# Delta-rule attention: scores taken out of the solve loop, computed in 32x64 array tiles over parity-masked keys, and kept raw in SBUF

## The chip, the cores and the metric

The kernel runs on one core of a Trainium2 chip. The metric is the device time of one execution in microseconds (us), as the median of several runs. TensorE multiplies matrices and writes to PSUM (8 banks of 512 float32 columns in 128 partitions); VectorE and ScalarE read PSUM and SBUF; GpSimd works on SBUF alone; SyncE issues transfers. The engines run side by side and wait for each other through semaphores.

## The reference, cut to what matters

The program is a decoder of two layers over 16 sequences of 64 tokens with 256 features. The change touches only the attention of the second layer, with 16 heads of 16 features, chunks of 16 positions and 64 positions in all:

```python
def step(S, inp):                       # one chunk of CHUNK positions (here all 64 of a sequence)
    K, V, bt = inp
    A = jnp.tril(jnp.einsum('bhik,bhjk->bhij', K, K) * bt[:, :, None, :], -1)
    rhs = V - jnp.einsum('bhck,bhkv->bhcv', K, S)
    Vn = jax.scipy.linalg.solve_triangular(eye + A, rhs, lower=True)
    ...
v, _state = _kernel_regression(k, v, beta)
k = k * beta[..., None]
scores = jnp.einsum('bqhd,bkhd->bhqk', q, k) * scale
scores = jnp.where(mask, scores, -jnp.inf)          # mask: lower triangle
attn = jax.nn.softmax(scores, axis=-1)
out = jnp.einsum('bhqk,bkhd->bqhd', attn, v).reshape(b, n, d)
return out @ Wo
```

So there are two things that meet only at the end: the triangular solve that makes the new values v, and the causal softmax over the scores of q and k, which needs nothing of the solve.

## The kernel before, in words

Everything is written by hand, engine by engine: each engine's code is a list of instructions in program order, with waits on semaphores, and nothing reorders it. Only the part between the turned queries and keys and the values is touched.

*Keys by keys.* TensorE turns queries and keys tile by tile (8 tiles of 128 tokens, two sequences each), ScalarE copies them out as `qt1` (queries) and `kbt1` (keys times beta), and TensorE multiplies keys by keys into the matrix of the solve, `na1`. While this goes on, VectorE scales the keys of the next tile (L2409, L2410), and copies half of the products. GpSimd makes the first three of the "keys by head" `kb1` (L737): a product of the keys with a head mask, eight heads wide, one for each of 16 work items w (w = 2j + k, tile j, feature half k), in three buffers.

*Inverses.* The 16x16 diagonal blocks are turned (L1327), copied out by ScalarE (L1918), and inverted by substitution (`invert1`, L416 and L418), half of them on VectorE, half on GpSimd, which first clears their place `ti1` (L754). Each half goes to memory and comes back in another layout (SyncE, L622 and L626). ScalarE fills two blocks of units into `na1` (L1927), GpSimd a third (L763).

*Solve loop.* 16 solve steps t (four chunks of 16 positions x four groups): `rest_of_chunk` (L1383, what earlier chunks give), `own_heads` on VectorE (a masked product), `solved_chunk` (L1397, times the inverse), then copies of the result back into `xv1`, three by ScalarE (L1945) and one by VectorE (L2446). Into the same loop are woven the 16 items of the softmax: `scores1` (L1350 puts the causal mask into a bank through a bf16 identity, L1353 adds the scores of 64 queries with eight heads wide of masked keys), `softmax1` on VectorE (maximum L2429 and subtraction L2430, both from PSUM), `exp1` on ScalarE (L1932), `turn_probs1` (L1362, four transposes) and `keep_probs` on ScalarE (L1939) into `pt1`. Four items run ahead of the loop, with matmuls that only keep TensorE's clock up (L816); scores use one bank, turned probabilities one.

*After the loop* TensorE puts the values in order (L1429) and multiplies probabilities by values (`values1`, L1444). Later the cross attention uses, for its own scores (`scores5`, L1478), tiles of 32 rows x 64 columns, 32 of them for a tile of tokens.

A float32 matmul stands as two records in the trace, so 16 records of L1383 are eight matmuls.

## Time and profile before

| | us |
|---|---|
| median of 3 runs | 1045.49 |
| lowest and highest of them | 1042.62 and 1056.3 |
| the profiled execution | 1040.52 |
| its span, first to last instruction | 1038.6 |
| TensorE (matmul) busy | 958.0 (92%) |
| VectorE busy | 541.3 (52%) |
| ScalarE busy | 362.9 (35%) |
| GpSimd busy | 213.7 (21%) |

Busy time is summed over stages that have different limits, so a share says little about one of them. A busy TensorE is also one whose matmuls only keep the clock up. The chain that ended last, 68% TensorE and 21% VectorE over the whole program, has to be read stretch by stretch; here the stretch is that from about 530 to 652 us.

### The profile page before, as it was taken

Reading aid. Unit: us, or ns where it says so; the run is one execution under the profiler, and the core shown is the slowest. Engines: PE = TensorE matmul, PEld = TensorE weight load, DVE = VectorE, ACT = ScalarE, POOL = GpSimd, SP = SyncE. Lnnn points to the kernel's source line nnn. Section 1 sums busy time; section 2 is a strip of 40 time slices with the busy share of each in tenths; the row PEclk is TensorE's granted clock in tenths of the full one; section 3 lists DMA queues with packets and bytes.
Section 4 is the critical chain, followed back from the end, with each engine's and each line's share of the span. In section 5 each row is a group of like instructions: output and inputs, shape, how many; then the busy total and the mean of one; then the engine's idle time right before and its main releaser. Section 6 shows DMA issues by size and latency. Waiting matters only on the chain.

```text
span 1038.6 us, 18579 instructions
## 1 busy us (share of the span) xinstructions
PE 958.0 (92%) x7302; PEld 594.0 (57%) x7302; DVE 541.3 (52%) x1083; ACT 362.9 (35%) x729; POOL 213.7 (21%) x259
## 2 busy tenths in 40 slices
PE   7799899999989999999888899878899999999995
PEld 3665543333458899997554467746554444444453
DVE  2589788988441110113788677758663232332325
ACT  2334536666522223333477245245230000000002
POOL 6011100000012222312125842730000111111110
PEclk9999999999989999999999999999799999999998
DMA  5000330000345555645130201230105033332001
GB/s 210 1 3 1 119 136 2 2 2 2 122 149 211 164 185 177 185 148 171 48 42 1 81 2 42 83 145 3 51 13 128 0 93 93 92 93 88 6 0 42
DMA packets 28602, 81.43 MB, mean 78 GB/s; under 512 B 10068, under 2 KB 17372, under 8 KB 22500
## 3 DMA queue, kind: packets, MB, share of 16 engines
q1 hardware_dynamic: 26308, 74.20, 21.9%
q0 software_dynamic: 2208, 6.03, 1.9%
q8 instruction: 60, 0.98, 0.4%
q14 instruction: 26, 0.21, 0.1%
HBM read 70.62 MB, written 8.55 MB: 76 GB/s over the span
## 4 chain that ended last, share of the span: by engine, by line
PE 68%; DVE 21%; ACT 4%; issue 3%; POOL 2%; DMA 1%; DVEq 0%; SPq 0%; ACTq 0%; POOLq 0%
PE psum L1588 9%; PE psum L1164 8%; PE psum L1176 8%; DVE arena L2185 5%; PE psum L1592 3%; PE psum L878 3%; PE psum L1383 3%; PE psum L1618 3%; PE psum L1576 3%; PE psum L1622 3%; PE psum L1554 2%; PE psum L1062 2%; DVE arena L2102 2%; DVE arena L2101 2%; PE psum L1613 2%
## 5 line engine op out<-in xcount | busy, mean ns | idle before, releaser
L2034 ACT ACTIVATE arena<-psum 128x512 f32<-128x512 f32 (+1 forms) x32 | 19.0, 593 | 219.5 <-PE psum L1592 219.5
L1842 ACT ACTIVATE arena<-psum,arena 128x128 f32<-128x128 f32 x184 | 52.4, 368 | 115.4 <-PE psum L1164 78.5
L1588 PE MATMUL psum<-arena 128*128 128x512 f32 (+1 forms) x192 | 90.6, 608 | 0.5 <-DVE arena L2653 0.5
L805 POOL TENSOR_TENSOR arena<-arena 128x512 f32<-128x512 f32 (+1 forms) x32 | 40.4, 1264 | 234.5 <-ACT arena L2034 234.5
L2185 DVE TENSOR_REDUCE arena<-psum 128x2 f32<-128x512 f32 x128 | 82.5, 688 | 11.0 <-PE psum L1008 9.5
L1164 PE MATMUL psum<-arena 128*128 128x128 f32 x736 | 86.8, 276 | 0.5 <-DVE arena L2328 0.5
L1164 PEld LDWEIGHTS psum<-arena 128*128 128x128 f32 x736 | 84.0, 192 | 3.4 <-issue 2.7
L1176 PE MATMUL psum<-arena 128*128 x368 | 83.4, 378 | 0.0
L2328 DVE COPY arena<-psum 128x256 f32<-128x256 f32 x23 | 9.7, 424 | 136.5 <-PE psum L1149 86.0
L1819 ACT ACTIVATE arena<-psum 128x1024 f32<-128x1024 f32 x64 | 65.3, 1024 | 30.4 <-PE psum L1030 27.1
L1176 PEld LDWEIGHTS psum<-arena 128*128 128x128 f32 x368 | 67.9, 189 | 9.0
L2653 DVE TENSOR_TENSOR arena<-arena,psum 128x512 f32<-128x512 f32 (+1 forms) x32 | 22.1, 689 | 86.9 <-POOL arena L805 86.4
L1588 PEld LDWEIGHTS psum<-arena 128*128 128x128 f32 (+1 forms) x192 | 33.1, 185 | 55.2 <-issue 53.5
L816 PE MATMUL psum<-arena 128*128 128x512 f32 (+1 forms) x118 | 50.9, 554 | 0.0
L1008 PE MATMUL psum<-arena 32*128 32x256 f16 x256 | 44.5, 276 | 5.8 <-DVE arena L2185 2.7
L728 POOL DMA_INDIRECT returned<-arena x23 | 22.7, 987 | 123.5 <-DVE arena L2344 123.5
L2636 DVE TENSOR_TENSOR arena<-psum,arena 128x512 f32<-128x512 f32 x32 | 22.1, 692 | 49.7 <-issue 45.8
L737 POOL TENSOR_TENSOR arena<-arena 128x512 f32<-128x512 f32 x32 | 32.9, 1054 | 45.9 <-ACT arena L1900 27.4
L878 PE MATMUL psum<-arena 64*128 64x256 f32 x256 | 33.1, 399 | 6.5 <-DVE arena L2132 5.9
L1062 PE MATMUL psum<-arena 128*32 128x256 f32 x512 | 35.1, 393 | 0.6 <-ACT arena L1819 0.5
L1592 PE MATMUL psum<-arena 64*128 64x512 f32 (+1 forms) x96 | 34.4, 625 | 0.0
L816 PEld LDWEIGHTS psum<-arena 128*128 128x128 f32 (+1 forms) x118 | 19.3, 169 | 26.2 <-issue 25.8
(357 smaller groups left out, 1764.2 us busy)
## 6 DMA issues: line engine op xcount, KB each, us to landing
arena<-in_w SPq DMA_DIRECT2D x31, 1024.0 KB, 9.9
arena<-in_experts SPq DMA_DIRECT2D x8, 1248.0 KB, 6.0
arena<-mixed SPq DMA_DIRECT2D x16, 256.0 KB
arena<-mixed SPq DMA_DIRECT2D x8, 512.0 KB, 9.3
arena<-returned SPq DMA_DIRECT2D x8, 256.0 KB, 4.5
kept<-arena SPq DMA_DIRECT2D x2, 1024.0 KB, 7.8
arena<-kept SPq DMA_DIRECT2D x2, 1024.0 KB, 5.9
arena<-in_w_ffn SPq DMA_DIRECT2D x1, 1152.0 KB, 5.1
```

Source lines behind the costliest of these rows:

```text
L805: do(pool.tensor_tensor(out=g6[rows, 2 * half + i, :], in0=g6[rows, 2 * half + i, :], in1=scale6[rows, f % BUFS, cols], op=ALU.mult), scaled6)
L816: pe.matmul(bank(spare), eye, wide(eye, 1, BANK // P), start=True, stop=True)
L878: last = pe.matmul(replicated(u, p)[:, g * D:(g + 1) * D], w[rows, g, :], qr[rows, u % 2, i, :], start=(i == 0), stop=(i == 1), tile_posit ...
L1008: last = pe.matmul(bank(u % 2)[:, tc * D:(tc + 1) * D], stack["q"][r0:r1, b, g, tc * P:(tc + 1) * P], stack["k"][r0:r1, b, g, :], start=Tr ...
L1062: last = pe.matmul(bank(6)[32 * q:32 * q + 32, 0:D], vx[:, b, sc, q, 32 * g:32 * g + 32], ptx[:, (n + q // 2) % 4, q % 2, sc, :], start=(g ...
L1164: last = pe.matmul(bank(n)[:, i * P:(i + 1) * P], w1_tile[:, r % 2, k, features], xst[:, r % 2, k, :], start=(k == 0), stop=(k == KC - 1))
L1176: last = pe.matmul(bank(4 + r % 2)[:, 0:D], hidt[:, r % 2, ic * P:(ic + 1) * P], w2v[:, bass.ds(e, 1), ic, :], start=(ic == 0), stop=(ic = ...
L1588: pe.matmul(out, e[w][:, k, :], xe6[:, half, k, :], start=(k == 0), stop=False)
L1592: mid_ps.by(pe.matmul(out, qb6[r0:r1, n // 2 % 2, q0:q0 + m], aw6[r0:r1, half, :], start=False, stop=True))
L1819: ptx_ready.by(act.activation(ptx[:, n % 4, :, :, :].rearrange("p a b c -> p (a b c)"), bank(2 + 2 * (n % 2), 2), ACT.Exp, scale=float(DHX ...
L1842: last = act.activation(hidt[:, r % 2, ic * P:(ic + 1) * P], bank(n)[:, i * P:(i + 1) * P], ACT.Gelu, bias=b1_tile[:, r % 4, ic:ic + 1])
L2185: ax_max.by(dve.tensor_reduce(nmx[:, b % 2, :, h], bank(u % 2).rearrange("p (t s) -> p t s", t=2), AX.X, ALU.max, negate=True))
```

## The change

Scores are now made two items at a time (n = 0 to 7, tile j), right after the diagonal blocks are out, in banks 0 to 5 by turns. Instead of keys masked by head and eight heads wide, GpSimd makes two copies of the keys, `kwp1[0]` and `kwp1[1]`, each masked by the parity of the head; an array tile of 32 feature rows holds two heads, and the parity picks one of them. A score is then a matmul of 32 rows, 64 queries and 64 keys, at a tile position of the array. ScalarE copies every bank of raw scores to SBUF (`raw1`): the second eight items into their own places of `pt1`, which are free by then, the first eight into the room beyond the arena and next to `xv1`. In the loop, VectorE takes maximum and subtraction from there, two items ahead; turned probabilities get two banks; the fourth copy of a solved chunk goes from VectorE to ScalarE; and GpSimd instead of ScalarE fills the unit block of chunk 2. The items are taken in the order 8 to 15, 0 to 7. The keep-clock matmuls of this stretch are gone.

```diff
+        kwp1 = [key_half(kw_at), key_half(ARENA + BEYOND - KC * B * S)]
+
+        def raw1(w):
+            if w >= NT:
+                return pt1[:, w, :]
+            at = ARENA + w * BANK if w < NT - 2 else xv1_at - (NT - w) * BANK
+            return arena.t[:, at:at + BANK]
...
-        GROUPS, EARLY_W = 4, 4
+        GROUPS, W_ORDER = 4, [*range(NT, 2 * NT), *range(NT)]
...
-            sp.wait_ge(a1_ps.sem, 2 * NT)
+            sp.wait_ge(a1_ps.sem, NT)
             sp.dma_start(w_x1, a["w_xattn1"]).then_inc(loaded["w_xattn1"].sem, 16)
...
+            def keys_by_parity(j):
                 pool.wait_ge(ft_sb.sem, 2 * j + 1)
...
+                for k in range(KC):
+                    for e in range(2):
+                        last = pool.tensor_scalar(
+                            kwp1[e][:, k, j * P:(j + 1) * P].rearrange("p (a i) -> p a i", i=CH),
+                            kbt1[k][:, 2 * j:2 * j + 2, :, 0:CH].rearrange("p b c i -> p (b c) i"),
+                            c["parity"][:, e:e + 1], None, ALU.mult)
                 kb1_ready.by(last)
...
-            for w in range(3):
-                keys_by_head(w)
+            for j in range(NT - 1):
+                keys_by_parity(j)
...
+            keys_by_parity(NT - 1)
             pool.wait_ge(nd1_sb.sem, nd1_sb.base + 2 * CHUNKS)
             invert1(pool, do, pool_step, 1)
...
-            for w in range(3, 2 * NT):
-                keys_by_head(w)
+            for chunk in (2, 3):
+                rows = slice(32 * chunk, 32 * chunk + 32)
+                do(pool.tensor_copy(na1[rows, chunk, :, :].rearrange("p u (h i) -> p (u h) i", i=CH),
+                                    wide(c["ident"][rows, 32 * chunk:32 * chunk + CH], 1, B * KC * 8)), unit_pool)
...
+                for g in range(2):
+                    pe.matmul(bank(2 * (n % 3) + g), ident1, wide(causal1, 1, 8), start=True, stop=False,
+                              skip_group_check=True)
+                for i in range(2):
+                    at = slice((2 * j + i) * S, (2 * j + i + 1) * S)
+                    for k in range(KC):
+                        for r in range(2):
+                            to = ((i * KC + k) * 2 + r) * S
+                            for quad in range(4):
+                                g, e = divmod(quad, 2)
+                                rows = slice(32 * quad, 32 * quad + 32)
+                                last = pe.matmul(bank(2 * (n % 3) + g)[64 * e:64 * e + 64, to:to + S], qt1[rows, k, at],
+                                                 kwp1[r][rows, k, at], start=False, stop=True,
+                                                 tile_position=(32 * quad, 64 * e), skip_group_check=True)
                 a1_ps.by(last)
...
-            for w in range(EARLY_W):
-                scores1(w)
-                if w == 0:
-                    keep_clock(16, 5)
-                if w >= 1:
-                    keep_clock(2, 5, ident1)
-                    turn_probs1(w - 1)
+            pe.wait_ge(causal_ready.sem, causal_ready.base + 1)
+            pe.wait_ge(nd1_sb.sem, nd1_sb.base + 2 * CHUNKS)
+            for n in range(NT):
+                scores1(n)
             pe.wait_ge(xv1_in.sem, xv1_in.base + 16 * 2 * CHUNKS)
+            pe.wait_ge(raw_sb.sem, raw_sb.base + 2 * NT)
             for t in range(SOLVES + 1):
-                w = EARLY_W + t
                 if t < SOLVES:
                     rest_of_chunk(t)
-                if w < 2 * NT:
-                    scores1(w)
                 if t >= 1:
                     solved_chunk(t - 1)
-                if w <= 2 * NT:
-                    turn_probs1(w - 1)
...
+                if t < SOLVES:
+                    turn_probs1(t)
...
+            act.wait_ge(xv1_in.sem, xv1_in.base + 16 * 2 * CHUNKS)
+            for n in range(2 * NT):
+                act.wait_ge(a1_ps.sem, n // 2 + 1)
+                raw_sb.by(act.activation(raw1(W_ORDER[n]), bank(2 * (n // 2 % 3) + n % 2), ACT.Copy))
+            act.wait_ge(gather_dve.sem, gather_dve.base + 4)
+            unit_act.by(act.activation(na1[32:64, 1, :, :].rearrange("p u (h i) -> p (u h) i", i=CH),
+                                       wide(c["ident"][32:64, 32:32 + CH], 1, B * KC * 8), ACT.Copy))
...
-                for q in range(3):
+                for q in range(4):
                     xv_act.by(act.activation(group_units(t, q)[32 * chunk:32 * chunk + CH],
...
+                if t < SOLVES:
+                    keep_probs(t)
+                if t + 2 < 2 * NT:
+                    exp1(t + 2)
...
+            for n in range(2):
+                softmax1(n)
+            for t in range(SOLVES):
+                own_heads(t)
+                if t + 2 < 2 * NT:
+                    softmax1(t + 2)
```

Where this puts the instructions: TensorE first, at the head of the solve loop. In these rows `wct_sb` is the semaphore of `own_heads`, `kb_ready` that of the copied `xv1`, `ceb_sb` that of the raw scores in SBUF (before: of VectorE's solved copy). Before, an iteration of the loop:

```order
L1383 MATMUL psum<-arena 128x128 [waits wct_sb]
L1383 MATMUL psum<-arena 128x128 x3
L1350 MATMUL psum<-arena 128x512 [waits sm_ready,kb1_ready]
L1353 MATMUL psum<-arena 64x512 x2
L1397 MATMUL psum<-arena 16x128 [waits wct_sb]
L1397 MATMUL psum<-arena 16x128 x3
L1362 MATMUL psum<-arena 128x128 [waits pt_sb,sm_exp]
L1362 MATMUL psum<-arena 128x128 x3
```

Now, from the last pair of scores (L1362 is now the mask, L1372 the tiles) into the loop (L1402 rest, L1382 turned probabilities, L1415 solved):

```order
L1362 MATMUL psum<-arena 128x512 [waits ceb_sb,kb1_ready]
L1362 MATMUL psum<-arena 128x512
L1372 MATMUL psum<-arena 64x64 x32
L1402 MATMUL psum<-arena 128x128 [waits ceb_sb,kb_ready]
L1402 MATMUL psum<-arena 128x128 x7
L1382 MATMUL psum<-arena 128x128 [waits sm_exp]
L1382 MATMUL psum<-arena 128x128 x3
L1402 MATMUL psum<-arena 128x128 x8
L1415 MATMUL psum<-arena 16x128 [waits wct_sb,tst1_in_0]
L1415 MATMUL psum<-arena 16x128 x3
```

The mask and the scores stand ahead of the loop, and an iteration is rest, solved, turned probabilities. Turned probabilities 0 now stand behind rest 0 and ahead of rest 1.

ScalarE from the copied diagonal blocks on. Before (L1918 diagonal blocks, L1927 units, L1932 exponentials, L1939 kept probabilities):

```order
L1918 ACTIVATE arena<-psum 128x4x4x16 [waits r1_ps] x8
L1927 ACTIVATE arena<-arena 32x4096 [waits yx_read]
L1927 ACTIVATE arena<-arena 32x4096 [waits yx_ps]
L1932 ACTIVATE arena<-arena 128x512 [waits sm_ready] x2
L1939 ACTIVATE arena<-psum 128x512 [waits pt_ps]
```

Now (L1930, L1936 raw scores, L1938 units, L1943 exponentials, L1950 kept probabilities, L1956 solved copies):

```order
L1930 ACTIVATE arena<-psum 128x4x4x16 [waits r1_ps] x8
L1936 ACTIVATE arena<-psum 128x512 [waits a1_ps,kb_ready]
L1936 ACTIVATE arena<-psum 128x512 [waits a1_ps] x15
L1938 ACTIVATE arena<-arena 32x4096 [waits yx_read]
L1943 ACTIVATE arena<-arena 128x512 [waits sm_ready] x2
L1950 ACTIVATE arena<-psum 128x512 [waits pt_ps]
L1943 ACTIVATE arena<-arena 128x512 [waits sm_ready]
L1956 ACTIVATE arena<-psum 16x2x128 [waits cnt_ps]
L1956 ACTIVATE arena<-psum 16x2x128 x3
```

Sixteen raw copies stand ahead of the one unit block that is left, and both ahead of the first exponential.

## Rows read from the trace of the kernel before

**Rows 1.** The chain in order of time: start us, us, engine, line, records.
```profile
600.42 1.98 PE psum L1383 x16
602.40 0.32 PE psum L1350
602.72 1.01 PE psum L1353 x4
603.73 0.56 PE psum L1397 x16
604.29 0.59 PE psum L1362 x4
...
631.03 1.79 PE psum L1383 x16
632.81 0.22 PE psum L1350
...
652.19 5.46 PE psum L1429 x64
```

**Rows 2.** Timeline of the inverses' time: start us, us, engine, line, operation, idle before.
```profile
559.90 7.27 ACT L1927 ACTIVATE arena<-arena 32x4096 f32<-32x4096 f32 x2
...
560.02 0.29 POOL L416 TENSOR_TENSOR arena<-arena 128x60 f32<-128x60 f32 x1 [8.03 <-ACT arena L1918]
560.02 0.38 PE L1350 MATMUL psum<-arena 128*128 128x512 bf16 x1 [1.12 <-ACT arena L1918]
...
561.33 14.00 PE L816 MATMUL psum<-arena 128*128 128x512 f32 x32
...
577.17 0.69 DVE L2430 TENSOR_TENSOR arena<-psum,arena 128x512 f32<-128x512 f32 x1
...
578.01 0.58 PE L1350 MATMUL psum<-arena 128*128 128x512 bf16 x1 [2.68 <-DVE arena L2430]
...
578.52 1.98 PE L1353 MATMUL psum<-arena 128*64 128x512 f32 x4
...
579.06 0.38 SPq L626 DMA_DIRECT2D arena<-inverse  x1
```

**Rows 3.** The two transfers of L626, from issue to landing.
```profile
DMA to landing us min/median/max: 4.2/4.3/4.3
```

**Rows 4.** Stretches: length, PE, PEld, DVE, ACT, POOL busy, granted clock, DMA.
```profile
578.00:579.00 1.00, 0.99 (x3) 0.37 (x5) 0.00 (x0) 0.53 (x1) 0.83 (x3) 0.53 0.52 213
582.00:583.00 1.00, 0.82 (x5) 0.29 (x5) 0.03 (x1) 0.94 (x2) 1.00 (x1) 1.00 1.22 327
```

**Rows 5.** ScalarE by shape, 560 to 655: count, busy us, mean ns, idle before.
```profile
L1945 ACT ACTIVATE arena<-psum 16x256 f32<-16x256 f32 x48 | 17.9, 374 | 27.9 <-PE psum L1397 27.1
...
L1932 ACT ACTIVATE arena<-arena 128x512 f32<-128x512 f32 x16 | 10.0, 624 | 18.5 <-DVE arena L2430 18.5
L1939 ACT ACTIVATE arena<-psum 128x512 f32<-128x512 f32 x16 | 9.5, 593 | 2.5 <-PE psum L1362 2.2
```

**Rows 6.** Timeline of the cross attention's scores, TensorE.
```profile
697.81 1.99 PE L1478 MATMUL psum<-arena 32*64 32x64 f32 x64
...
705.92 1.16 PE L1478 MATMUL psum<-arena 32*64 32x64 f32 x64
```

**Rows 7.** Timeline while keys are turned; last row: GpSimd by shape, 500 to 560.
```profile
531.34 6.50 POOL L737 TENSOR_TENSOR arena<-arena 128x512 f32<-128x512 f32 x6 [27.43 <-ACT arena L1900]
...
535.00 0.75 DVE L2409 TENSOR_TENSOR arena<-arena 128x256 f32<-128x256 f32 x1
...
535.78 1.15 DVE L2410 TENSOR_TENSOR arena<-arena 128x256 f32<-128x256 f32 x1
...
538.29 0.42 DVE L2409 TENSOR_TENSOR arena<-arena 128x256 f32<-128x256 f32 x1
...
547.15 1.80 POOL L754 MEMSET arena<- 128x2048 f32 x1 [9.32 <-PE psum L1292]
...
L749 POOL CAST arena<-arena 128x128 bf16<-128x128 f32 x1 | 0.3, 289 | 0.1
```

More of the change, by code:

```diff
@@ L339, in build @@
         kbt1 = [arena.take(B, CHUNKS, 32), ctok.rearrange("p j d -> p (j d)").rearrange("p (b c i) -> p b c i", c=CHUNKS, i=32)]
[L340 removed]
+        kw_at = arena.at
+        arena.take(3, 2, 8, S)
         xv1_at = arena.at
@@ L729, in _ @@
                                             ys[:, q % 2, :], None).then_inc(ys_out[q % 2].sem, 16)
-            def keys_by_head(w):
-                j, k = divmod(w, 2)
+            def keys_by_parity(j):
                 pool.wait_ge(ft_sb.sem, 2 * j + 1)
-                if w >= 3:
-                    pool.wait_ge(a1_ps.sem, w - 2)
-                for i in range(2):
-                    b = 2 * j + i
-                    last = pool.tensor_tensor(out=kb1[:, w % 3, i, :, :].rearrange("p h (c i) -> p h c i", i=CH),
-                                              in0=wide(kbt1[k][:, b, :, 0:CH], 1, 8),
-                                              in1=wide(wide(c["headmask1"], 2, CH), 2, CHUNKS), op=ALU.mult)
+                for k in range(KC):
[4 more added lines that the diff above has]
+                            c["parity"][:, e:e + 1], None, ALU.mult)
                 kb1_ready.by(last)
@@ L1355, in scores1, with turn_probs1 @@
                 a1_ps.by(last)
-            def turn_probs1(w):
-                pe.wait_ge(sm_exp.sem, w + 1)
-                if w >= 1:
-                    pe.wait_ge(pt_sb.sem, w)
+            def turn_probs1(n):
+                pe.wait_ge(sm_exp.sem, n + 1)
+                if n >= 2:
+                    pe.wait_ge(pt_sb.sem, n - 1)
                 for i in range(4):
-                    last = pe.transpose(bank(7)[:, i * P:(i + 1) * P], sm1[:, w % 2, i * P:(i + 1) * P],
+                    last = pe.transpose(bank(6 + n % 2)[:, i * P:(i + 1) * P], sm1[:, n % 2, i * P:(i + 1) * P],
@@ L2421, in _, with softmax1 @@
             invert1(dve, do, dve_step, 0)
-            def softmax1(w):
-                dve.wait_ge(a1_ps.sem, w + 1)
-                if w >= 2:
-                    dve.wait_ge(pt_ps.sem, w - 1)
-                sm = sm1[:, w % 2, :].rearrange("p (h t) -> p h t", t=S)
-                scores = bank(6).rearrange("p (h t) -> p h t", t=S)
-                do(dve.tensor_reduce(mx1[:, w % 2, :], scores, AX.X, ALU.max))
-                do(dve.tensor_tensor(out=sm, in0=scores, in1=wide(mx1[:, w % 2, :], 2, S), op=ALU.subtract),
+            def softmax1(n):
+                dve.wait_ge(raw_sb.sem, raw_sb.base + n + 1)
+                if n >= 2:
+                    dve.wait_ge(pt_ps.sem, n - 1)
+                sm = sm1[:, n % 2, :].rearrange("p (h t) -> p h t", t=S)
+                scores = raw1(W_ORDER[n]).rearrange("p (h t) -> p h t", t=S)
+                do(dve.tensor_reduce(mx1[:, n % 2, :], scores, AX.X, ALU.max))
+                do(dve.tensor_tensor(out=sm, in0=scores, in1=wide(mx1[:, n % 2, :], 2, S), op=ALU.subtract),
                    sm_ready)
```

100 lines of the change are left out of this document (30 added, 70 removed).

## Prediction

> **What bounds the kernel now.** I read the chain that ended last in order of time, then the timeline of the same stretch, then groups by shape. In the solve loop, which ends where L1429 starts at 652.19 us, the chain is TensorE without a gap: every iteration is five pieces that follow each other [rows 1]. An early one is 1.98 (L1383, the rest of a chunk) + 0.32 (L1350, the causal term) + 1.01 (L1353, the scores) + 0.56 (L1397, the solved part) + 0.59 (L1362, the turned probabilities) = 4.46 us. From the chunk with 96 rows on, L1383 is 1.79 and L1350 0.22, so 4.16. ScalarE and VectorE are not the bound there: per iteration they run three L1945 copies, one L1939 and one L1932 (3 x 0.37 + 0.59 + 0.62 = 2.3 us) [rows 5], and four operations of 0.69 such as L2430 [rows 2] with one short copy.
>
> Before the loop TensorE has nothing useful to do: it does scores 0 at 560.02, then 14.00 us of keep-clock matmuls (L816), sits 2.68 us idle, and comes back only when VectorE has finished its inverse and the first softmax [rows 2]. So the place of free TensorE time is 561 to 578, and the place where TensorE is short is the loop. The change moves work from the second to the first.
>
> **The change, part by part.**
>
> *Scores out of the loop.* Twelve iterations lose L1350 + L1353: eight of 1.33 and four of 1.23 us, 15.6 us of pure path. The four scores ahead of the loop, with their turns, also go; what takes their place is worked out below as a timetable.
>
> *Scores in the new form.* A pair of old scores becomes two L1350 and 32 tiles of 32 rows x 64 columns. The trace has this tile form in the cross attention (L1478, 64 records for 32 tiles): 1.16 us at full clock, 1.99 at a low one [rows 6]. A pair is 0.32 + 0.22 + about 1.1 = 1.65 us, against 2 x 1.33 before. Eight pairs from 560.02 (the wait for L1918's last copy is unchanged) end at 573.2. Their three pairs of banks are emptied by ScalarE at 2 x 0.59 = 1.2 us a pair [rows 5], less than 1.65, so it keeps up; the last two copies end at 574.4, and TensorE waits for them.
>
> The Trainium skill, "TensorEngine Tiling (Array Packing)", Restrictions and Gotchas, says that different row tiles cannot access one PSUM bank simultaneously; here two row tiles share each bank, in different partition halves. By the 1.01 us of L1353 for 512 columns a tile of 64 is 0.11 to 0.13; if the two on a bank took turns, I estimate 16 x 0.11 = 1.7 us instead of 1.1 for the tiles of a pair, turn 1 would end 3 us later, and the sum below would give about 19 us instead of 22. L1478 writes its banks in the same way and shows 1.16, so by the row I leave the turn-taking out; what no row shows is the same form accumulating on top of L1350's result.
>
> *Start of the loop.* Rest 0 runs 574.4 to 576.4; it needs neither inverse nor softmax. VectorE's inverse 0 is unchanged, and so its first maximum starts behind it and its first subtraction ends at 577.86 as before [rows 2]. ScalarE does the unit block of chunk 1 first, 3.6 us (half of the 7.27 of two), so it is free at 578.0; exp 0 ends at 578.6. TensorE has then been idle for 2.2 us. Before, after an idle 2.68 us, it came back at 1.2 GHz (granted clock 0.53 at 578 to 579, 1.00 from 582), and L1353 took 1.98 instead of 1.01 [rows 2, 4]. I take the same: turn 0 to 579.8, rest 1 to about 583. Solved 0 needs the first inverse back from memory: its load is issued at 579.06 and lands 4.3 us later, at 583.4 [rows 2, 3]. So the slow clock is covered by that wait, and solved 0 (0.56) and turn 1 (0.59) end at 584.6.
>
> *The loop.* Then rest + solved + turn: 1.98 + 0.56 + 0.59 = 3.13 us for t = 2 to 7 (18.8), and 1.79 + 1.15 = 2.94 for t = 8 to 14 (20.6); rest 15 and solved 14 another 2.35: 626.3. Behind it ScalarE has four copies, one keep of probabilities, four copies: 8 x 0.39 + 0.6 = 3.8 us, so L1429 starts at 630.1. Before it starts at 652.19 [rows 1]. **The sum is 22.1 us.**
>
> *Who else could set the pace.* ScalarE now has 4 x 0.39 + 0.61 + 0.64 = 2.8 us an iteration, since the fourth copy came over from VectorE. VectorE has 4 x 0.72 = 2.9. Both lie just under 2.94. The margin is thin, but what they feed has slack: softmax t+2 and exp t+2 have two iterations, a solved chunk's copy has four. If waits between engines make either 3.2 long, the loop loses about 0.2 x 14 = 3 us.
>
> *Reading raw scores from SBUF.* No row shows a VectorE maximum or subtraction of 128x512 from there; PSUM sources cost 0.69 each. I take 0.69 for both. Above it lies what VectorE showed beside GpSimd, next part; below zero nothing speaks for.
>
> *Keys by parity.* GpSimd makes them in 28 pieces of 128x128 while the queries are turned (531 to 547) and four more at about 552, and does nothing for them in the loop. The six old products took 6.50 us there, 1.08 each for 512 elements of two inputs; a quarter of that is 0.27, and a GpSimd cast of 128x128 took 0.29 [rows 7]. I take 0.3, 28 pieces 8.4 us, and call 0.6 the upper end. The clearing of ti1 (L754) waited 9.32 us and the inverse behind it another 8.03 [rows 2, 7], so up to 0.6 a piece this is covered; above it inverse 0 would be pushed. But VectorE's two scaling products (L2409, L2410), 0.42 each when left alone, took 0.75 and 1.15 at 535, when GpSimd was at its six products [rows 7]. That cost 1.06 us, on the chain. Now GpSimd works through that whole phase in short pieces. If every pair of VectorE's seven later products lost 1.06, that is 7.4 us; if a short piece blocks only briefly, the 1.06 comes back. I take nothing, and both ends go into the range.
>
> The Trainium skill, "SBUF — State Buffer", Who interferes with whom, says that a VectorE operation with two SBUF inputs contends with a GpSimd instruction that reads SBUF, whole instruction by whole instruction, and one with a single SBUF input does not. The rows at 535 agree. By this rule the new subtraction, now with both inputs in SBUF, contends too: softmax 2 and 3 fall on GpSimd's two unit blocks (3.6 us each from 579.5), and I estimate up to 2 us of delay for each, which the wait for the inverse and the slack of two iterations would hide.
>
> *SyncE.* The next stage's weights wait for a1_ps at half the count, so they load before the loop instead of near its end, behind the inverse's loads. Nobody waits for them either way. Nothing downstream of L1429 changes.
>
> **Rivals.**
> - *Slow tiles.* The scores run at the low clock or take turns on the banks. At half clock a pair is 1.99 [rows 6] and about 0.9 for the two L1350, 2.9 us; eight end at 583.2, their copies at 584.4, the unit block at 588.0, turn 0 at 589.3, and the loop's regular part starts 8 us later: 14 us of gain, 1031. Against it: the keep-clock matmuls are replaced by work that is as dense, and L1478 at full clock.
> - *VectorE or ScalarE sets the pace*, by contention with GpSimd in the key phase (up to 7.4) or the thin margin in the loop (3): gain 12 to 19, about 1029. For it: the 0.75 and 1.15, and 2.9 against 2.94.
> - *Slower than before.* TensorE stays at 1.2 GHz after the idle time ahead of turn 0, through the loop. All of the 43 us at half speed cost 43, so the time would be 1045.5 + 21; it decides once more than 44 us of half-speed work, some 22 us lost, come together. Against it: in the trace of before full clock was back by 582 with TensorE far from full.
> - *More than the sum*: the 1.06 comes back and the inverse lands earlier: 25 us or more, below 1020.
>
> **How the numbers follow.** The profiled execution took 1040.5 us (span 1038.6), so the sum gives 1018.4 for it. The median shown is 1045.49, 5 us above; I take the gain off that: 1023. Chances: the forecast (gain 18.5 to 25, 1020 to 1027) 0.65; slow tiles 0.10; another engine sets the pace 0.17; slower 0.03; more than the sum 0.05. Two per cent, about what a measurement of this kernel can tell from no change, are 20.9 us, 1024.6: just beside the forecast. Of the forecast's 0.65 I put 0.45 above it, since the sum is 22.1 with few free terms; with the last case that is 0.50 faster, 0.46 within, 0.04 slower. The range 1017 to 1032 leaves out the slower case, the worst of the contention and noise of the median.
>
> **What would show it.** In the profile after: eight pairs of L1350's successor and 32 tiles at 1.65 us from 560 to 573; an idle TensorE at 576 to 578.6 with a granted clock near 0.5 behind it; solved 0 waiting for the load until 583.4; iterations of 3.13 and 2.94 with no gap; L1429's successor at 630. Wrong would be: tile groups of 1.7 us or more, VectorE's products at 533 to 546 well above 0.42, subtractions above 0.69, or idle TensorE in the loop.

## The result, and the profile after

The changed kernel takes 1043.44 us (median of 18 runs, 1035.80 to 1048.67); the kernel before, run in turn with it, takes 1048.30 (18 runs, 1042.46 to 1056.30). The ratio is 0.9949, with an interval of 0.9924 to 0.9974. So the change gains half a per cent, about 5 us; the forecast was 22. The profiled execution of the new kernel took 1043.96 us (span 1042.0), 3.4 us more than that of the kernel before.

The page gives the span's TensorE at 92% busy, and the mean granted clock fell from 0.974 to 0.942. The slices of PEclk say where: a 7 and a 5 stand at slices 23 and 24, that is from 573 to 625 us.

```profile
PEclk9969998999989999999899759999799999999998
```

Before comparing stretches, one thing has to be taken out. The code ahead of the key scaling is the same in both kernels, yet it ended at 528.7 us in the trace of before and at 538.7 in that of after. TensorE was at the low clock there for longer, in places such as 50 to 70 us (the columns are length, busy time of PE, PEld, DVE, ACT and POOL with counts, granted clock, DMA share, GB/s). After:

```profile
50.00:60.00 10.00, 10.00 (x86) 8.08 (x82) 5.08 (x7) 2.45 (x7) 0.00 (x0) 0.50 0.01 2
```

and before:

```profile
50.00:60.00 10.00, 10.00 (x150) 8.73 (x147) 7.37 (x12) 3.61 (x11) 2.46 (x4) 0.88 0.01 2
```

This varies between executions of one kernel: in the two later profiles of variants of the kernel before (below) the same code ended at 536.0 and 536.1. It goes far to explain why the times of each kernel spread over 13 us, and it is why this case is read by stretches and not by spans. From the start of the key scaling on:

| Stretch | before | after | forecast |
|---|---|---|---|
| key scaling to first mask matmul | 31.3 | 29.3 | 31.3 |
| first mask matmul to first output matmul (L1429, now L1441) | 92.2 | 88.5 | 70.1 |
| from there to the end | 386.4 | 385.5 | 386.4 |

The middle stretch holds the missing 18.4 us. Its window row before, and after:

```profile
560.00:652.20 92.20, 86.74 (x696) 53.16 (x696) 66.72 (x105) 43.13 (x82) 51.48 (x60) 0.98 0.13 37
```

```profile
568.00:656.50 88.50, 81.50 (x1105) 66.65 (x1105) 61.95 (x89) 55.27 (x113) 29.89 (x35) 0.75 0.15 42
```

The whole stretch was to be 70.1 us, and TensorE alone is busy for 81.5 of it: the granted clock is 0.75 against 0.98. The chain of after in order of time shows it piece by piece (start, length, engine, line, records):

```profile
568.03 0.59 PE psum L1362 x2
568.62 1.09 PE psum L1372 x64
...
582.49 1.09 ACT arena L1936 x2
583.60 3.62 ACT arena L1938
587.24 0.64 ACT arena L1943
587.92 1.11 PE psum L1382 x4
589.03 3.71 PE psum L1402 x16
592.74 0.98 PE psum L1415 x16
593.72 1.05 PE psum L1382 x4
594.77 3.71 PE psum L1402 x16
...
629.21 2.28 PE psum L1402 x16
...
637.92 0.59 PE psum L1382 x4
638.51 1.79 PE psum L1402 x16
```

The order is that of the forecast: scores, last raw copies, unit block, exponential 0, turned probabilities 0, rest 1. But an iteration of the loop is 3.71 + 0.98 + 1.05 = 5.74 us where 1.98 + 0.56 + 0.59 = 3.13 was expected, with no gap in it. Every piece runs at half clock, until the chunk with 96 rows (from 629): there they are 1.79 + 0.56 + 0.59, exactly as forecast. The windows show the fall and the return:

```profile
585.00:586.00 1.00, 0.73 (x7) 0.54 (x5) 0.96 (x2) 1.00 (x1) 0.87 (x2) 0.88 0.69 283
586.00:587.00 1.00, 0.00 (x0) 0.00 (x0) 0.93 (x3) 1.00 (x1) 0.84 (x3) 0.50 0.60 242
...
600.00:601.00 1.00, 1.00 (x5) 0.67 (x4) 0.35 (x1) 0.95 (x3) 0.00 (x0) 0.50 0.80 336
629.00:630.00 1.00, 1.00 (x6) 1.00 (x6) 0.66 (x1) 0.93 (x4) 0.00 (x0) 0.50 0.00 0
630.00:631.00 1.00, 1.00 (x11) 1.00 (x10) 0.93 (x3) 0.64 (x2) 0.00 (x0) 0.94 0.00 0
```

The clock falls to 1.2 GHz and stays there for some 44 us, through a loop in which TensorE is busy all the time. The row of 585 to 586 places the fall: 1.00 for 0.76 of the microsecond and 0.50 behind it, so it came at 585.8. That is just as rest 0 ended, and ahead of nearly all of the 2.19 us in which TensorE waits for the exponential:

```profile
583.72 2.02 PE L1402 MATMUL psum<-arena 32*128 32x128 f32 x16 [1.30 <-ACT arena L1936]
587.92 1.11 PE L1382 MATMUL psum<-arena 128*128 128x128 f32 x4 [2.19 <-ACT arena L1943]
```

What lay ahead of the fall was the wait of 1.30 us for the last raw copies and 2.02 us of matmuls with 32 rows. Before, the clock was back by 582, within 4 us of the end of its wait [rows 4].

### The profile page after: what moved, and what is told of

The parts are those of the page before. It is cut to its first block, busy times and chain, and to the rows that moved or that the text cites. A ratio compares the mean times of both kernels' runs of the same rounds, so it can differ in the third digit from the quotient of the medians.

```text
span 1042.0 us, 19365 instructions
## 1 busy us (share of the span) xinstructions
PE 963.9 (92%) x7712; PEld 613.9 (59%) x7712; DVE 533.0 (51%) x1067; ACT 375.3 (36%) x760; POOL 205.8 (20%) x260
## 4 chain that ended last, share of the span: by engine, by line
PE 73%; DVE 18%; ACT 5%; issue 3%; DMA 1%; POOL 0%; SPq 0%; DVEq 0%; ACTq 0%; POOLq 0%
PE psum L1600 8%; PE psum L1178 8%; PE psum L1190 8%; DVE arena L2193 5%; PE psum L1402 4%; PE psum L1604 3%; PE psum L892 3%; PE psum L1630 3%; PE psum L1588 3%; PE psum L1634 3%; PE psum L1076 2%; PE psum L1566 2%; DVE arena L2110 2%; DVE arena L2109 2%; PE psum L1625 2%
## 5 line engine op out<-in xcount | busy, mean ns | idle before, releaser
L1600 PE MATMUL psum<-arena 128*128 128x512 f32 (+1 forms) x192 | 90.6, 608 | 0.5 <-DVE arena L2651 0.5
L1600 PEld LDWEIGHTS psum<-arena 128*128 128x128 f32 (+1 forms) x192 | 33.1, 185 | 55.2 <-issue 53.5
L1402 PE MATMUL psum<-arena 32*128 32x128 f32 (+3 forms) x256 | 44.6, 344 | 1.3 <-ACT arena L1936 1.3
L1402 PEld LDWEIGHTS psum<-arena 32*128 32x128 f32 (+3 forms) x256 | 41.8, 254 | 3.7 <-issue 2.4
L1076 PE MATMUL psum<-arena 128*32 128x256 f32 x512 | 38.4, 422 | 0.6 <-ACT arena L1831 0.5
L892 PE MATMUL psum<-arena 64*128 64x256 f32 x256 | 32.7, 395 | 6.5 <-DVE arena L2140 5.9
L830 PE MATMUL psum<-arena 128*128 128x512 f32 (+1 forms) x80 | 34.6, 545 | 0.0
```

The costliest lines, as they stand in the source:

```text
L892: last = pe.matmul(replicated(u, p)[:, g * D:(g + 1) * D], w[rows, g, :], qr[rows, u % 2, i, :], start=(i == 0), stop=(i == 1), tile_posit ...
L1076: last = pe.matmul(bank(6)[32 * q:32 * q + 32, 0:D], vx[:, b, sc, q, 32 * g:32 * g + 32], ptx[:, (n + q // 2) % 4, q % 2, sc, :], start=(g ...
L1402: last = pe.matmul(bank(n % 4)[:, q * P:(q + 1) * P], lhs, xv1[rows, u, :], start=True, stop=True)
L1600: pe.matmul(out, e[w][:, k, :], xe6[:, half, k, :], start=(k == 0), stop=False)
```

## The experiments

What stays open after this comparison is whether the clock is the whole of the missing gain, and why it doesn't come back. Rows are here the partitions of the two operands, the first number of a form such as 32*128; columns are those of the moving operand. Two explanations: the work of the first chunks (L1402 with 32 or 64 rows, L1415 and L1382 with 128) can't raise the clock however densely it is fed; or the idle time before the loop did the damage and any dense feed would mend it. All experiments but two start from the changed kernel. Each run has a label, given again where it is discussed. The columns are the three stretches of the table above and the clock of the middle one, each from one profiled execution.

| | key to mask | mask to output | to the end | clock |
|---|---|---|---|---|
| before | 31.3 | 92.2 | 386.4 | 0.98 |
| after | 29.3 | 88.5 | 385.5 | 0.75 |
| e1_fill | 29.3 | 74.9 | 385.5 | 0.98 |
| e2_rows128 | 29.3 | 70.0 | 386.7 | 0.98 |
| e3_exp_first | 29.2 | 87.9 | 386.9 | 0.75 |
| e4_before_no_keep | 31.3 | 91.8 | 389.4 | 0.91 |
| e5_no_idle | 29.3 | 86.9 | 386.8 | 0.80 |
| e7_burst | 29.3 | 81.4 | 388.3 | 0.90 |
| e8_zero_rows | 29.3 | 70.3 | 387.4 | 1.00 |
| e9_burst32 | 29.2 | 97.9 | 385.4 | 0.70 |
| e10_burst64 | 29.3 | 96.6 | 387.4 | 0.72 |
| e6_keys_late (of before) | 31.8 | 93.5 | 387.6 | 0.96 |

**Filling the wait (e1_fill).** Seven keep-clock matmuls of 128 rows and 512 columns stand between rest 0 and turned probabilities 0.

```diff
             for t in range(SOLVES + 1):
                 if t < SOLVES:
                     rest_of_chunk(t)
+                if t == 0:
+                    keep_clock(7, 5)
```

> The changed kernel with one addition: seven keep-clock matmuls (512 columns, 128 rows, float32) between rest 0 and turned probabilities 0, where TensorE stood idle for 2.19 us before its clock fell to 1.2 GHz at 585.9 us and stayed there until 630. Theory A (the idle time loses the clock, and the thin work of the first two chunks cannot bring it back): the clock stays at 2.4 GHz through the loop, iterations are 3.13 us from the start, and the stretch from the first scores to the ordering of the values is 70 to 72 us instead of 88.5; the time falls 15 to 19 us below the changed kernel. Rival B (the work of the first two chunks cannot even hold the clock): the clock falls inside the loop although nothing was idle, and the stretch stays above 80 us.

Measured: 1026.58 us (6 runs, 1022.89 to 1033.86) against 1051.23 of before (11 runs); ratio 0.980, 0.9745 to 0.9855. The stretch is 74.9 us. The timeline of TensorE in this kernel (start, length, engine, line, operation, count):

```profile
580.10 7.90 PE L830 MATMUL psum<-arena 128*128 128x512 f32 x14
...
588.37 2.05 PE L1402 MATMUL psum<-arena 32*128 32x128 f32 x16
```

and its windows:

```profile
580.00:581.00 1.00, 1.00 (x3) 0.50 (x2) 0.94 (x2) 1.00 (x1) 0.92 (x2) 0.50 0.79 311
...
584.00:585.00 1.00, 1.00 (x4) 0.52 (x3) 0.00 (x0) 0.00 (x0) 1.00 (x1) 1.00 0.61 142
...
600.00:632.00 32.00, 32.00 (x391) 27.96 (x381) 28.54 (x43) 27.94 (x66) 4.40 (x3) 1.00 0.01 2
```

The fill was too long: it ended at 588.0, where turned probabilities 0 could have started at 582.1 (19.9 us behind the first mask matmul, as in after), and the stretch is 4.8 us above the forecast's 70.1 (70 to 72 had been expected of this run). The loop behind it runs at full clock, rest by rest 2.05 us, so with the clock up nothing else limits it: neither ScalarE nor VectorE. But the clock still fell, at 580.0, as rest 0 was ending and the fill began, so the empty place behind rest 0 can't have been what made it fall; the expectation, which puts the 2.19 us of idle time ahead of the fall, has the order wrong. It came back within the fill. The thin loop (rests of 32 and 64 rows) holds a high clock; it didn't need to raise one here.

**The same loop with all rows (e2_rows128).** The rest of every chunk reads all 128 rows (this adds foreign terms to the remainders, so it is for the time alone).

```diff
-                rows = slice(0, 32 * (chunk + 1))
+                rows = slice(0, P)
```

> The changed kernel with one change: the rest of a chunk always reads all 128 rows, in the first chunk instead of 32 and in the second instead of 64 (it then adds terms that do not belong there, so its output differs). Number, columns and order of the matmuls are the same, the idle time ahead of turned probabilities 0 stays. Theory A in the form that rows count (few rows of the array in use do not bring the clock back): the clock falls at the idle time and is back at 2.4 GHz within two iterations, by about 600 us, and the stretch from the first scores to the ordering of the values shrinks from 88.5 to 74 to 78 us. Rival C (the return has to do with elapsed time or with something outside TensorE's work): low for 40 us as before, 88 us.

Measured: 1019.78 us (one run), stretch 70.0. The number of instructions and their columns are unchanged; only the rows of the operands are more. The clock fell at 581.2, here at the end of the 2.18 us of wait, but came back during rest 1, less than 3 us behind its start:

```profile
581.11 1.08 PE L1382 MATMUL psum<-arena 128*128 128x128 f32 x4 [2.18 <-ACT arena L1943]
581.98 3.19 PE L1402 MATMUL psum<-arena 128*128 128x128 f32 x16
```

Windows of the same kernel:

```profile
582.00:583.00 1.00, 1.00 (x6) 1.00 (x6) 0.89 (x2) 0.60 (x1) 1.00 (x1) 0.50 1.08 246
584.00:585.00 1.00, 1.00 (x8) 0.99 (x7) 1.00 (x1) 0.00 (x0) 1.00 (x1) 0.71 0.85 328
585.00:586.00 1.00, 1.00 (x21) 0.68 (x20) 0.96 (x2) 0.32 (x1) 0.94 (x2) 1.00 0.09 33
```

This is the forecast's picture, wait and dip included. That the stretch agrees with the forecast to 0.1 us is in part luck: the score tiles take 1.2 us more than forecast (below), and the rests of the first two chunks take less with 128 rows than with 32 or 64 (1.95 us against 2.05 in the timelines, an iteration 2.93 against 3.13). The chain that ended last runs through VectorE in this run, 2.90 us an iteration, so the margin that the prediction called thin is used up, without an idle TensorE in the loop to show for it.

**Moving or closing the idle time (e3_exp_first, e5_no_idle).** First ScalarE's exponentials 0 and 1 ahead of its unit block (L1938), so that turned probabilities 0 come earlier:

```diff
-            act.wait_ge(gather_dve.sem, gather_dve.base + 4)
-            unit_act.by(act.activation(na1[32:64, 1, :, :].rearrange("p u (h i) -> p (u h) i", i=CH),
-                                       wide(c["ident"][32:64, 32:32 + CH], 1, B * KC * 8), ACT.Copy))
...
             for n in range(2):
                 exp1(n)
+            act.wait_ge(gather_dve.sem, gather_dve.base + 4)
...
```

> The changed kernel with one change: ScalarE does the first two exponentials ahead of its unit block of 3.62 us instead of behind it. Turned probabilities 0 then start about 1.3 us after rest 0 has begun to wait instead of 2.2 us, but rest 1 is done earlier and TensorE then waits for the inverse's load, 1.5 to 2.5 us. Theory A: the idle time is only moved, so the clock falls here too, and the stretch stays at 83 to 89 us. If it does not fall, the stretch is about 71 us and the order on ScalarE was the cause.

Measured: 1045.17 us (one run), stretch 87.9. The idle time ahead of turned probabilities 0 went from 2.19 to 1.34 us, and the clock fell all the same and stayed down:

```profile
588.00:630.00 42.00, 42.00 (x262) 34.63 (x262) 25.05 (x33) 23.82 (x45) 8.15 (x4) 0.50 0.22 64
```

Then the same with short fills in each wait:

```diff
+            keep_clock(2, 7)
             pe.wait_ge(xv1_in.sem, xv1_in.base + 16 * 2 * CHUNKS)
...
                     rest_of_chunk(t)
+                if t < 2:
+                    keep_clock(1 + t, 5)
```

> The changed kernel with every idle stretch at the head of the loop cut or filled: ScalarE does the first two exponentials ahead of its unit block, and TensorE does two keep-clock matmuls (0.88 us each) while the last raw scores are copied, one behind rest 0 and two behind rest 1. Nothing thin or idle is then longer than about 2 us. Theory A: the clock is high from the first scores to the values, the loop's regular part starts when the inverse lands, and the stretch is 70 to 71 us against 88.5 of the changed kernel and 74.9 with seven matmuls behind rest 0; ratio to before 0.975 to 0.98. If the clock falls all the same, by rest 0 alone, and nothing dense follows that is long enough, the stretch is 85 to 88.

Measured: 1034.45 us (median of six runs, 1022.83 to 1041.91) against 1046.25 of before (11 runs). The stretch of the profiled run (1036.23) is 86.9, where 70 to 71 was expected. What idle time was left is the wait for the first inverse; the clock fell 2.2 us behind its end, at 587.4, while TensorE was busy, and stayed down until the third chunk:

```profile
585.20 0.63 PE L1415 MATMUL psum<-arena 128*16 128x128 f32 x16 [1.18 <-DMA arena<-inverse]
...
586.35 2.81 PE L1402 MATMUL psum<-arena 32*128 32x128 f32 x16
```

The two fastest runs (1022.83 and 1023.73) have no trace. But with the shortest other stretches of any profile here (528.7, 29.2 and 385.4) their spans of 1020.9 and 1021.8 leave at most 78.5 us for the middle one, an estimate from these rows, so the loop can't have been low for as long as in the profiled run. So fills around the waits kept most of the loss away in some executions and not in others.

**A burst inside the slow loop (e7_burst, e9_burst32, e10_burst64)**, of 128, 32 and 64 rows. Four keep-clock matmuls behind rest 2, when the clock is already down (the other two runs pass `ident[0:32, :]` and `ident[0:64, :]` as operands):

```diff
                     rest_of_chunk(t)
+                if t == 2:
+                    keep_clock(4, 5)
```

> The changed kernel with four keep-clock matmuls inside iteration 2 of the loop, where nothing was idle and the clock had been low for over 10 us. Theory A (dense work brings it back, thin work then holds it): 1.2 GHz from the idle time until the burst, 2.4 from its end to the end of the loop; the burst itself costs 5 to 7 us, the remaining five low iterations give back 2.6 us each, 13 us; the stretch is 79 to 83 us. If thin work cannot hold it, the clock falls again within the next iterations and the stretch is 92 or more.

> The changed kernel, with four keep-clock matmuls of 512 columns behind the third part of the remainders (the second chunk's first), as in the burst run, but with the first 32 rows of the unit matrix as both operands in place of all 128 (lhsT 32 x 128, moving side 32 x 512). The burst of 128 rows found the clock at 0.50 and left it at 1.00. Theory A (the rows that stream through the array count, not how densely TensorE is fed): the burst passes in about 7 us at 0.50 throughout and the iterations behind it stay at 0.50 until the third chunk; the stretch from the first mask matmul to the start of the output is 88.5 + 4 x 0.875 to 4 x 1.75 us, about 92 to 96 us. Theory B (an unbroken feed with long matmuls is enough, whatever the rows): the clock is at 1.00 behind the burst, as with 128 rows, and the stretch is 79 to 83 us. If the clock never falls in this execution the run tells nothing.

> As the run before it, with the first 64 rows. This places the number of rows from which the clock comes back: by the rests of the changed kernel, 64 rows did not bring it back in the second chunk and 96 rows did at the start of the third. Theory A: 64 rows behave as 32, stretch 92 to 96 us, 0.50 until the third chunk. Theory B: clock at 1.00 behind the burst, 79 to 83 us.

Measured (one run each): 1031.78, 1054.76 and 1046.69 us; stretches 81.4, 97.9 and 96.6. The windows of the burst with 128 rows:

```profile
594.00:596.00 2.00, 2.00 (x4) 0.84 (x3) 0.00 (x0) 0.00 (x0) 0.00 (x0) 0.50 0.00 0
596.00:598.00 2.00, 2.00 (x7) 0.52 (x6) 0.00 (x0) 0.00 (x0) 0.00 (x0) 0.66 0.00 0
598.00:600.00 2.00, 2.00 (x28) 1.62 (x28) 0.66 (x1) 1.25 (x4) 0.00 (x0) 1.00 0.00 0
600.00:610.00 10.00, 10.00 (x116) 8.50 (x115) 8.86 (x14) 8.51 (x20) 0.00 (x0) 1.00 0.01 2
```

of that with 32 rows:

```profile
602.00:604.00 2.00, 2.00 (x4) 0.87 (x3) 0.00 (x0) 0.00 (x0) 0.00 (x0) 0.50 0.06 25
606.00:640.00 34.00, 34.00 (x215) 27.76 (x215) 15.87 (x23) 16.36 (x36) 0.00 (x0) 0.50 0.00 1
```

and of that with 64:

```profile
594.00:596.00 2.00, 2.00 (x4) 0.93 (x3) 0.00 (x0) 0.00 (x0) 0.00 (x0) 0.50 0.03 12
600.00:630.00 30.00, 30.00 (x189) 24.74 (x188) 14.51 (x22) 14.87 (x34) 0.00 (x0) 0.50 0.00 1
```

Three bursts with the same instructions, columns and unbroken feed, all met at 0.50. The one of 128 rows leaves the clock at 1.00, and the iterations of 32 and 64 rows behind it hold it there. Those of 32 and 64 rows pass in 7.0 and 7.2 us and change nothing. That an unbroken feed is enough falls by these runs. The stretches with 32 and 64 rows are 2 and 0.6 us above the 92 to 96 expected; with 32 rows the clock came back only 7 us into the third chunk (in after 1 us, in the run with 64 rows 3 us).

But 64 rows are no bar in themselves. At about 50 us, in code that nobody touched, every profile but that of the filled kernel has a fall, and the work behind it is of 64 rows (L892, L900 and L907 in the changed kernel). In the run with the 64-row burst the clock was back at 51.8 us with nothing but such work since the fall:

```profile
47.96 3.39 PE L892 MATMUL psum<-arena 64*128 64x256 f32 x16 [2.38 <-DVE arena L2142]
```

```profile
51.00:52.00 1.00, 1.00 (x12) 0.71 (x10) 1.00 (x1) 0.69 (x2) 0.00 (x0) 0.59 0.00 0
52.00:53.00 1.00, 1.00 (x23) 1.00 (x20) 0.96 (x2) 0.55 (x2) 0.00 (x0) 1.00 0.00 0
```

Five of the eleven profiles with this fall (before and the runs with all rows, with short fills and with bursts of 128 and 64 rows) show that quick return; the other six, after among them, stayed low for 20 us or more, busy nearly all the time with the same instructions. In the five the fall came by 49.0 us, with most of the time to the return still filled by L892 (256 columns); in the six it came between 49.4 and 50.5, nearer to L907 (64 columns). And 128 rows are no warrant: in after, matmuls of 128 rows and 64 columns (L1644) and transposes of 128x128 (L840) ran from 744 to 752 us, busy for 7.86 of 8 us, at 0.50:

```profile
749.22 3.51 PE L1644 MATMUL psum<-arena 128*128 128x64 f32 x16
750.00:752.00 2.00, 2.00 (x11) 2.00 (x10) 0.00 (x0) 1.15 (x1) 0.00 (x0) 0.50 0.96 404
```

So the bursts, one run each, separate 128 rows from 32 and 64 for matmuls of 512 columns in this place; a number of rows from which the clock returns they don't give.

**Rows of zeros (e8_zero_rows).** The first chunk's rests (0 to 3) read all 128 rows of `spread1`, of which rows 32 to 127 are cleared, so the sum doesn't change:

```diff
+            do(pool.memset(spread1, 0.0))
...
-                rows = slice(0, 32 * (chunk + 1))
+                rows = slice(0, 32 * (chunk + 1)) if chunk else slice(0, P)
```

> The changed kernel with one change: the rest of the first chunk reads all 128 rows of the spreading matrix, whose rows 32 to 127 GpSimd has cleared. Same number and columns of matmuls, nothing filled. The clock still falls at the idle time ahead of turned probabilities 0. Theory A in the form that rows in use count, whatever is in them: it is back within the first two or three iterations, as in the run with 128 rows of data, and stays there through the second chunk; stretch 70 to 73 us. If only rows with nonzero data count: low until the third chunk, 88 us.

Measured: 1024.31 us (6 runs, 1015.77 to 1026.04) against 1046.25 of before (11 runs); ratio 0.976, 0.9712 to 0.9808. The stretch is 70.3. The waits are all still there, and the clock doesn't fall in the profiled execution (busy time of PE first, granted clock third from the end):

```profile
582.00:584.00 2.00, 0.30 (x3) 0.11 (x1) 1.90 (x4) 1.98 (x2) 1.76 (x4) 1.00 0.63 262
586.00:588.00 2.00, 0.93 (x9) 0.74 (x7) 1.97 (x2) 0.00 (x0) 2.00 (x1) 1.00 1.24 313
```

It is faster than the kernel before by 22 us and than the changed one by about 19 (medians, the two measured at different times), for one clearing on GpSimd that nothing waits for. Its slowest run is below the fastest of the changed kernel. Whether the rows kept the clock from falling or only brought it back at once, these runs don't separate: in the run with all rows TensorE did the same until rest 1, and there the clock fell at the end of the 2.18 us of wait and was back within 4 us. What both have in common is that it did not fall during rest 0 or at its end, as it did in after, in the filled kernel and in the runs with bursts of 32 and 64 rows, where rest 0 has 32 rows. That is no proof: with exponentials first and with the burst of 128 rows, rest 0 has 32 rows too, and the clock fell in the wait behind it.

**What the removed keep-clock matmuls had bought (e4_before_no_keep).** The kernel before without them (L816 among the early scores):

```diff
                 scores1(w)
-                if w == 0:
-                    keep_clock(16, 5)
                 if w >= 1:
-                    keep_clock(2, 5, ident1)
                     turn_probs1(w - 1)
```

> The kernel before, without the keep-clock matmuls between its four early scores. TensorE is then idle for about 15 us ahead of scores 1 and its clock is low when the loop begins. Theory A: the loop of before, whose iterations also hold a 512-column mask matmul and 512-column scores over 128 rows, brings the clock back in its first two or three iterations although its rests use 32 rows too; the stretch from the first scores to the ordering of the values is 92.2 plus 4 to 8 us. Rival C: the clock stays low for tens of us here as well, and the stretch is over 110 us.

Measured: 1050.25 us (one run), stretch 91.8 where 96 to 100 was expected. TensorE then idles for 16.6 us and starts at the low clock, and dense scores of 512 columns bring it back within some 3 us, ahead of the loop:

```profile
588.00:590.00 2.00, 1.37 (x7) 0.68 (x7) 1.24 (x2) 0.69 (x2) 2.00 (x1) 0.81 1.21 280
590.00:592.00 2.00, 1.39 (x8) 0.42 (x4) 1.06 (x2) 0.42 (x1) 1.92 (x3) 1.00 0.46 184
```

So the missing keep-clock matmuls are not the cause: what the kernel before had at this place, and the changed one hasn't, are L1350 and L1353, with 128 rows and 512 columns each (the form of L1353 is 128*64: 64 is its width in the weights). Since the clock was back ahead of the loop, this run doesn't show whether the old loop, with L1350 and L1353 between its thin rests, could have raised it.

**Where the 2 us in the key phase come from (e6_keys_late).** In the kernel before, the three `keys_by_head` products of GpSimd are moved behind the clearing and filling of `ti1`, so that they no longer lie beside VectorE's scaling:

```diff
-            for w in range(3):
-                keys_by_head(w)
             pool.wait_ge(tr1_ps.sem, 2 * NT)
...
+            for w in range(3):
+                keys_by_head(w)
             pool.wait_ge(nd1_sb.sem, nd1_sb.base + 2 * CHUNKS)
```

> The kernel before with one change: GpSimd makes its first three keys by head behind the clearing of the inverses' place instead of ahead of it, so it does nothing while VectorE scales the keys. If the 2.0 us that the changed kernel gained between the first scaled keys and the first scores (29.3 instead of 31.3) came from VectorE's two products no longer standing behind GpSimd's long products, this stretch is 29.3 to 30.3 us here too, and the two products take 0.42 instead of 0.75 and 1.15. If it stays at 31.3, the gain came from somewhere else.

Measured: 1050.92 us (one run); the first stretch is 31.8 us, where 29.3 to 30.3 would have confirmed the guess. The contention on the products is gone, all 16 take 0.42 or 0.43. But VectorE's two pairs of copies within `na1` (`gather`, L2403) now take 3.95 and 3.96 us, beside GpSimd's clearing and products, where before they were 3.88 and 2.48: the loss moved from one VectorE line to the next.

## Why the prediction was right and wrong

**The failed step is "Start of the loop"**, and in it one sentence: "I take the same: turn 0 to 579.8, rest 1 to about 583", with the clock back by 582 as in [rows 4] and the low stretch covered by the wait for the inverse. Turned probabilities 0 met the low clock as said, though the fall came at the end of rest 0 and not in the idle time that the prediction gave as its cause: in part right by luck. The return did not come. It was carried over from a stretch, 578 to 581.5 us of before, in which all of TensorE's work had 128 rows (L1350, L1353, L816, L1362), and the change takes all of it but the transposes (L1362, now L1382) from this place; what follows the wait now is rests of 32 rows. In place of "back by 582" the runs showed a clock at 1.2 GHz for 44.4 us, until the chunk with 96 rows. The 128-row burst, the rests with 128 rows and the third chunk agree: in these runs TensorE came back to 2.4 GHz while it worked on operands of 96 or 128 rows (after 1 to 7 us), and never, in 30 us or more, while it worked on rests of 32 or 64 rows with L1415 and L1382 between them, though it was busy all the time. Why rests of few rows don't bring it back stays open: the returns at 50 us with 64 rows and the low 128-row stretch at 750 us show that rows are not the whole of it.

The Trainium skill, "TensorE: Matmul & The Clock Gate", "What's actually happening", says that the gate goes by how busy the array has been, and that activity releases the throttle. With "busy" read as time at work, the trace doesn't agree: TensorE was busy for 42.00 of 42 us at 0.50 in the run with the exponentials first.

**The sum of the loss.** Counted from the first mask matmul: rest 2 starts 26.7 us behind it (forecast 24.6); of the 2.1 us, 1.3 lie ahead of turned probabilities 0 (nearly all in two pairs of score tiles that paused, below), 0.9 are the slow solved 0 and turned probabilities 1. Six iterations at 5.74 in place of 3.13 are 15.7. The third and fourth chunks with the tail take 27.3 against 26.7. That makes 18.4, the whole of 88.5 − 70.1. With the clock up the stretch is 70.0 and 70.3 (128 rows, zero rows), so nothing else of weight was missing.

**The rivals.** The case called "slower than before" had the right mechanism, TensorE at 1.2 GHz through the loop, and was given 3 in 100 on the ground that full clock was back by 582 "with TensorE far from full" in the trace of before. That is a misreading: from 578 to 582 TensorE was busy for 3.96 of 4 us there (0.99 stands in [rows 4] itself; the 0.82 is behind the return), and the prediction doesn't ask what it was working on. Its price was too high too: it let the low clock go on to the end of the loop (43 us more), while the chunk with 96 rows ended it. "Slow tiles": the pairs take 0.54 + 1.09 = 1.63 us (1.65 forecast), at full clock. The rule of the Trainium skill on row tiles and PSUM banks ("TensorEngine Tiling (Array Packing)", Restrictions and Gotchas), which would have made it 1.7 for the tiles alone, shows no cost here: two row tiles write one bank, on top of L1362's result, at 1.09 us for 64 records. "Another engine sets the pace": with the clock up the iterations are 3.13 us (in the filled kernel rests start at 594.62, 597.74 and 600.87) and 2.94, without a gap.

**The other terms.** The eight pairs took 14.4 us and not 13.2: two of them, with pauses of 0.26 and 0.48 us between tiles that the trace puts down to the issue itself, took 2.20 and 2.33 instead of 1.63. The tail of ScalarE is 3.8 us as forecast, and rest 0, the unit block and the exponential took 2.02, 3.62 and 0.64. The raw scores read from SBUF cost VectorE 0.69 for the maximum. The subtraction took 2.54 us once, beside GpSimd's unit blocks; the timeline of after:

```profile
588.29 7.61 POOL L779 COPY arena<-arena 32x4096 f32<-32x4096 f32 x2
589.16 0.69 DVE L2437 TENSOR_REDUCE arena<-arena 128x8 f32<-128x512 f32 x1 [0.17 <-PE psum L1382]
589.89 2.54 DVE L2438 TENSOR_TENSOR arena<-arena 128x512 f32<-128x512 f32 x1
```

Both its inputs and that of GpSimd's copy are in SBUF. That is the contention cited ahead of the result, "SBUF — State Buffer", Who interferes with whom, in the Trainium skill, and its delay was hidden, as estimated there.

**Keys by parity** was mis-sized. A piece is 0.59 us (the median of 32), not 0.3; the 28 of the key phase take 0.656 on average, since single ones are held up (the longest took 2.55 us, beside VectorE's `gather` copies), and that is above what the prediction called the upper end (0.6):

```profile
541.37 18.36 POOL L748 TENSOR_SCALAR arena<-arena 128x128 f32<-128x128 f32 x28 [29.04 <-ACT arena L1912]
559.68 1.80 POOL L766 MEMSET arena<- 128x2048 f32 x1
```

It cost nothing: GpSimd still waited 0.99 us for ScalarE before its part of the inverse. And the phase got 2.0 us shorter where the prediction took 0. The products next to the pieces took 0.43 to 0.56, not 0.75 and 1.15 [rows 7], which is 0.8 us. The other 1.25 is VectorE's first pair of `gather` copies, now 2.63 us against 3.88: the late pieces push the clearing of `ti1` to 559.68, behind it. The run with the products moved shows such a copy at 3.95 beside GpSimd's clearing again, so this is a matter of what happens to lie side by side. The smaller part of that gain was among the cases ("the 1.06 comes back"), the larger wasn't seen.

## What to carry over

When a change takes wide matmuls out of a loop, ask of the rest of the loop whether it can bring TensorE's clock back after a fall, and look for a stretch in the trace with the same work at the low clock, not only for one with the same idle time. Where a loop of few rows follows a wait, try letting the first matmuls behind it read all 128 rows, the unneeded ones cleared: it cost no TensorE time and was worth 19 us here. The one long fill came close (ratio to before 0.980 against 0.976, with overlapping intervals), the short ones gained 12 us at the median, and not in every execution. When code that nobody touched differs by 10 us between two profiles, compare stretches from a common mark.

## What the hardware showed that was not expected

- TensorE at 1.2 GHz for 42 us at 100% busy, in a loop whose rests have 32 and 64 rows (L1415 and L1382 between them have 128); bursts of 7 us with 32 and 64 rows did nothing, one of 6.65 us with 128 rows brought 2.4 GHz back, and the thin loop then kept it.
- Rows of zeros did as well as others: with rows 32 to 127 cleared the clock of the profiled run was at 1.00 through waits of 1.30, 2.18 and 1.27 us, and all six runs (1026.04 at most) lie below the eighteen with 32 rows (1035.80 at least).
- What decides the fall isn't settled. It came during rest 0 (runs with bursts of 32 and 64 rows, 1.0 to 1.3 us behind the wait of 1.30), as rest 0 ended (after, filled kernel), while TensorE stood still (with exponentials first, with the burst of 128 rows) and 2.2 us behind a wait of 1.18 us (with short fills). The same code falls in one execution and not in another, at about 50 us too. No run here separates the share of the waits from that of the thin work around them.
- A GpSimd multiplication by a column of 128x128 float32 takes 0.59 us; a VectorE copy of 32x2048 within SBUF took 1.22 us at the least and up to 2.36 beside GpSimd's clearing (before, L2403).
